# Convolution in 64x64 tiles, pair 0's centring in its weights and its y on VectorE, ssm stage by token halves, new order

## The reference

```python
y = ln_last(x) @ inproj_w                       # per position, over the 64 channels
y = depthwise_conv_3x3(y, dw2d_w) + dw2d_b      # nine taps, zero padding
s = concat([raster, reversed raster, column, reversed column] of y)
r = ln_last(s) @ ssm_in_w.T ; a, g = split(r)   # 64 -> 2 x 128
r = depthwise_conv_1x3(a * sigmoid(g), ssm_dw_w) @ ssm_out_w.T
ys = nan_clean(r) + s
m = mean of the four directions, put back in raster order
x = nan_clean(m @ outproj_w) + x
x = attention(x)     # k and v normalised per head of 4, k^T v per image, gelu of a projection
x = moe(x)           # 8 experts, hidden 256, top 2 by softmax of the gate logits
```

## Time and profile before

| | us |
|---|---|
| median of 3 runs | 89.28 (89.16 to 90.37) |
| the profiled execution, first to last instruction | 88.6 |
| PE busy | 80.8 |
| ACT busy | 58.2 |
| DVE busy | 52.4 |
| POOL busy | 23.5 |

### The profile page before, as it was taken

One profiled execution on the slowest core, in us unless ns is written; L12 is line 12 of the kernel. 1 busy time (PEld: TensorE's weight loads), 2 busy tenths in 40 slices (PEclk: granted clock), 3 DMA queues, 4 the chain that ended last, 5 costly groups with the idle time before them and its releaser, 6 DMA issues.

```text
span 88.6 us, 1470 instructions
## 1 busy us (share of the span) xinstructions
PE 80.8 (91%) x439; PEld 55.0 (62%) x439; DVE 52.4 (59%) x160; ACT 58.2 (66%) x129; POOL 23.5 (26%) x50
## 2 busy tenths in 40 slices
PE   4999998979999999799997999999999969999950
PEld 1589886548575443486783688767885638556620
DVE  3002978567996768425876768993162968036390
ACT  4547935799854766769899998954981738700910
POOL 5758000401251520600030000320004502817700
PEclk9999999999999999999999999999999999999999
DMA  0899600000000000000000000000166100355011
GB/s 19 192 391 420 281 0 0 0 0 0 0 4 4 7 0 0 0 0 0 0 7 0 0 0 0 0 0 7 40 190 189 62 0 11 115 201 162 0 59 59
DMA packets 2647, 5.36 MB, mean 60 GB/s; under 512 B 432, under 2 KB 1104, under 8 KB 2512
## 3 DMA queue, kind: packets, MB, share of 16 engines
q1 hardware_dynamic: 2496, 5.19, 17.1%
q10 hardware_dynamic: 144, 0.09, 0.4%
HBM read 4.98 MB, written 0.29 MB: 60 GB/s over the span
## 4 chain that ended last, share of the span: by engine, by line
PE 59%; DVE 11%; ACT 8%; DMA 7%; issue 5%; POOL 3%; SPq 2%; POOLq 2%; DVEq 0%
PE psM L962 7%; PE psA L773 5%; DMA wbc<-gate_mem 5%; PE psB L682 4%; PE psT L692 3%; PE psT L711 3%; DVE prod L1375 2%; PE psA L797 2%; PE psB L806 2%; PE psA L799 2%; PE psA L798 2%; PE psB L808 2%; PE psB L810 2%; PE psA L946 2%; SPq L255 2%
## 5 line engine op out<-in xcount | busy, mean ns | idle before, releaser
L558 ACT ACTIVATE hs<-psA,early 128x512 f32<-128x512 f32 x16 | 11.1, 695 | 9.0 <-PE psA L947 6.6
L962 PE MATMUL psM<-hs,w_sb 128*64 128x256 f32 x128 | 14.9, 383 | 0.1
L962 PEld LDWEIGHTS psM<-hs,w_sb 128*64 128x64 f32 x128 | 8.8, 137 | 5.8 <-issue 1.4
L558 ACT ACTIVATE hs<-psB,early 128x512 f32<-128x512 f32 x16 | 11.1, 695 | 0.0
L1375 DVE SCALAR_TENSOR_TENSOR prod<-psM,early,wbc 128x256 f32<-128x256 f32 x16 | 7.0, 475 | 6.6 <-PE psM L962 4.7
L375 POOL TENSOR_TENSOR acc<-acc,prod 128x512 f32<-128x512 f32 x5 | 6.4, 1284 | 6.2 <-DVE prod L1375 5.8
L682 PE MATMUL psB<-warm 128*128 128x512 bf16 x16 | 5.4, 489 | 1.1 <-DVE warm L1080 1.1
L946 PE MATMUL psA<-xh,w_hl 128*128 128x512 f32 x14 | 5.9, 423 | 0.0
L946 PE MATMUL psB<-xh,w_hl 128*128 128x512 f32 x14 | 5.5, 393 | 0.0
L947 PE MATMUL psA<-xl,w_hl 128*128 128x512 f32 x14 | 5.5, 392 | 0.0
L947 PE MATMUL psB<-xl,w_hl 128*128 128x512 f32 x14 | 5.5, 391 | 0.0
(11 more groups left out here) (238 smaller groups left out, 195.3 us busy)
## 6 DMA issues: line engine op xcount, KB each, us to landing
wbc<-gate_mem SPq DMA_DIRECT2D x16, 128.0 KB, 3.1
w_nat<-in_w_dram SPq DMA_DIRECT2D x1, 1024.0 KB, 7.5
late<-in_late_dram SPq DMA_DIRECT2D x1, 616.0 KB, 5.5
w_sb<-in_w_dram SPq DMA_DIRECT2D x1, 512.0 KB, 8.3
ssm_in<-in_ssm_dram SPq DMA_DIRECT2D x1, 320.0 KB, 4.2
x_sb<-in_x_chan_dram SPq DMA_DIRECT2D x2, 128.0 KB, 2.4
out_dram<-fin SPq DMA_DIRECT2D x2, 128.0 KB, 1.7
early<-in_early_dram ACTq DMA_DIRECT2D x1, 89.5 KB, 2.6
```

The costliest lines, as they stand in the source:

```text
L558: nc.scalar.activation(hs[:, n % RING, :], hidden_bank(n), ACT.Gelu, bias=cols(V_B1 + n % (E * CK))).then_inc(S["h_ok"], 1)
L962: m = nc.tensor.matmul(psM[q * C:(q + 1) * C, bank, c0:c0 + L], w2_sb[:, s % (E * CK), :], hs[:, s % RING, q * L:(q + 1) * L], start=(k == ...
```

## The change

- The convolution is done wholly in PE: nine taps for each pair, each tap as four matmuls of 64x64 with 128 columns: rows by image q, output partitions by token half t. The tap weights are no longer made on ACT as five diagonals; DVE makes `taps_c` and `taps_y`, 128x576 each, from two 64x64 unit blocks.
- Pair 0's taps have the centring in them (`taps_c`). ACT squares the convolution's result with the centred bias `conv_bc` (`conv_squares`), and `conv_normalise` on DVE writes `norm_c`. The product `centered(1, 0)` is gone. Pair 0's y, which `outproj_y(0)` still needs, is made by DVE with nine taps (`conv_tap`), spread over its list.
- Pair 1's result goes to `y_sb` by ACT (`conv_out_y`) and is centred by a product as before. Its `outproj_y(1)` becomes four tiled matmuls.
- norm_c has token half t by channel in its partitions and (image, 128 tokens) in its columns, so the ssm products, sigmoids, `gated_u` and `raster` go by token halves instead of images.
- `keep_clock(7)` moves from the first place to behind `in_product(0)`.
- The lists of all four compute engines are put in a new order, and `column` and `kv_bias_parts` are split into parts so that other work can stand between.

The core of the diff:

```diff
+            def conv_squares():
+                act.wait_ge(S["conv_ps"], 4)
+                act.wait_ge(S["bc_ok"], 1)
+                nc.scalar.activation(by_half(cen_sq[:, 0, :]), conv_banks(0), ACT.Square, bias=conv_bc[:, :])\
+                    .then_inc(Q["sq_ok"][0], 1)
+            def conv_out_y():
+                act.wait_ge(S["conv_ps"], 8)
+                act.wait_ge(S["convb_ok"], 1)
+                nc.scalar.activation(by_half(y_sb[:, 1, :]), conv_banks(1), ACT.Identity, bias=conv_b[:, :])\
+                    .then_inc(S["y_ok"], 1)
...
             in_weights()
-            conv_diagonal(0)
-            conv_diagonal(1)
+            center_squares(0, 0)
             in_bias()
-            center_squares(0, 0)
             z_weights()
             center_squares(0, 1)
             rsqrt(0, 0, LN_EPS_CONV)
-            conv_diagonal(2)
+            gate_high()
             rsqrt(0, 1, LN_EPS_CONV)
-            conv_diagonal(3)
-            conv_diagonal(4)
-            ssm_biases()
+            conv_center_bias()
+            key_norm_diagonals()
+            w1_high(0)
             ssm_weights()
-            center_squares(1, 0)
+            conv_squares()
+            conv_out_y()
             rsqrt(1, 0, LN_EPS_CONV)
             center_squares(1, 1)
-            w1_high(0)
+            ssm_biases()
+            query_weights()
             rsqrt(1, 1, LN_EPS_CONV)
...
             head_rstd(1)
             first_token_rsqrt()
+            second_half_copies()
+            query_out(1)
+            token_high(0, 0)
+            token_high(0, 1)
             nc.scalar.preload_act_table_set("gelu_and_others")
-            query_out(1)
-            second_half_copies()
-            token_high(0, 0)
             heads_with_projection(1)
-            token_high(0, 1)
-            w1_high(3)
-            proj_gelu(1)
             hidden_gelu(0)
             hidden_gelu(1)
+            proj_gelu(1)
...
+                w = (taps_c, taps_y)[h]
+                for k in range(first, last):
+                    dy, dx = divmod(k, 3)
+                    for q in range(2):
+                        rows = slice(q * C, (q + 1) * C)
+                        for t in range(T):
+                            m = nc.tensor.matmul(conv_banks(h)[t * C:(t + 1) * C, q, :].rearrange("p (y x) -> p y x", x=W),
+                                                 w[rows, k, :],
+                                                 zpad[rows, h, dy + t * H // T:dy + (t + 1) * H // T, dx:dx + W],
+                                                 start=(k == 0), stop=(k == TAPS - 1))
...
             pe.wait_ge(S["warm_ok"], 1)
-            keep_clock(7, psB[:, 0, :])
             in_bias_product()
             centered(0, 0, x_sb)
             z_weight_product()
             centered(0, 1, x_sb)
             variance(0, 0)
+            conv_bias_product()
+            variance(0, 1)
             in_product(0)
+            keep_clock(7, psB[:, 0, :])
             in_product(1)
-            variance(0, 1)
-            ssm_bias_products()
-            convolution(0, 0, 3)
-            convolution(0, 3, 5)
+            convolution(0, 0, 9)
             convolution(1, 0, 3)
-            centered(1, 0, y_sb)
-            convolution(1, 3, 5)
+            convolution(1, 3, 6)
+            convolution(1, 6, 9)
             variance(1, 0)
             centered(1, 1, y_sb)
-            outproj_y(0)
+            ssm_bias_products()
+            query_transpose()
             variance(1, 1)
             ssm_products(0)
             centered_input(0)
+            key_norm_rows()
             ssm_products(1)
             raster(0, 0)
-            query_transpose()
             raster(0, 1)
-            column(0)
+            column(0, 0, 1)
+            column(0, 1, 2)
+            column(0, 2, 3)
+            outproj_y(0)
             raster(1, 0)
             raster(1, 1)
+            column(1, 0, 1)
             outproj(0, 0)
             outproj(0, 1)
-            column(1)
-            key_norm_rows()
+            column(1, 1, 2)
+            column(1, 2, 3)
+            outproj_y(1)
             centered_with_output(0)
-            outproj_y(1)
+            outproj(1, 0)
             variance(2, 0)
-            outproj(1, 0)
             outproj(1, 1)
+            centered_input(1)
...
             output(0)
             output(1)
             output(2)
+            hidden(5)
             gate_rows(0)
             token_copies(1, 0)
             token_copies(1, 1)
-            hidden(5)
...
             output(3)
             output(4)
             output(5)
-            output(6)
-            output(7)
             gate_rows(1)
             hidden(11)
             hidden(12)
             hidden(13)
+            output(6)
+            output(7)
...
+            conv_weights(True)
+            weight_sums()
             z_out(0)
-            conv_tap(0, 0)
-            conv_tap(1, 0)
+            kv_weights()
+            conv_weights(False)
+            kv_bias_parts(0, 1)
+            conv_tap(0)
+            conv_tap(1)
             z_out(1)
...
+            conv_tap(2)
+            conv_tap(3)
+            kv_bias_parts(1, 2)
+            conv_tap(4)
+            kv_bias_parts(2, 3)
+            conv_tap(5)
+            kv_bias_parts(3, 4)
+            conv_normalise()
+            conv_tap(6)
             normalise(1, 1, norm_c)
...
             largest(1)
-            gated_pair(0)
-            gated_pair(1)
+            gated(0)
+            gated(1)
             second(1)
             gate_parts(1)
+            gated(2)
+            gated(3)
+            gated(4)
             rows_out(1)
```

More of the change, by code:

```diff
@@ L68, in conv_attention_moe @@
         psM = ps("psM", [P, PAIRS, 512])
-        psA = ps("psA", [P, PAIRS, 512])
-        psB = ps("psB", [P, PAIRS, 512])
+        psAB = ps("psAB", [P, PAIRS, 2, 512])
+        psA, psB = psAB[:, :, 0], psAB[:, :, 1]
         early = sb("early", [P, P + NVEC])
@@ L752, in in_product, with conv_bias_product @@
                              .then_inc(S["z_ps"], 1)
+            def conv_bias_product():
+                pe.wait_ge(S["convb_ok"], 1)
+                pe.wait_ge(S["center_ok"], 1)
+                nc.tensor.matmul(psB[:, 1, 4:5], center[:, :], conv_b[:, :], start=True, stop=True).then_inc(S["bc_ps"], 1)
             def ssm_bias_products():
@@ L769, in convolution @@
                     pe.wait_ge(S["border_ok"], 2)
-                for i in range(first, last):
-                    dy, dx = divmod(PE_TAPS[i], 3)
-                    pe.wait_ge(S["diag_ok"], i + 1)
-                    m = nc.tensor.matmul(psA[:, h, 0:L].rearrange("p (y x) -> p y x", x=W), conv_diag[:, i, :],
-                                         zpad[:, h, dy:dy + H, dx:dx + W], start=(i == 0), stop=(i == len(PE_TAPS) - 1))
-                if last == len(PE_TAPS):
-                    m.then_inc(S["conv_ps"], 1)
+                    pe.wait_ge(S["taps_ok"], 3 + h)
+                w = (taps_c, taps_y)[h]
[8 more added lines that the diff above has]
+                                                 start=(k == 0), stop=(k == TAPS - 1))
+                            if k == TAPS - 1:
+                                m.then_inc(S["conv_ps"], 1)
             def ssm_products(h):
@@ L783, in ssm_products @@
                 for g in (1, 0):
-                    for q, bank in enumerate((psA, psB)):
-                        rows = slice(q * C, (q + 1) * C)
-                        m = nc.tensor.matmul(bank[:, h, g * L:(g + 1) * L], ssm_w[rows, g, q, :], norm_c[rows, h, :],
+                    for t in range(T):
+                        rows = slice(t * C, (t + 1) * C)
+                        m = nc.tensor.matmul(psAB[:, h, t, g * L:(g + 1) * L], ssm_w[rows, g, t, :], norm_c[rows, h, :],
                                              start=True, stop=True)
```

293 lines of the change are left out of this document (161 added, 132 removed).

## The result

The changed kernel takes **92.81 us** (median of 4 runs, 92.13 to 93.22) against 89.66 for the kernel before (4 runs, 89.16 to 90.37): a ratio of 1.032, 95% interval 1.025 to 1.039. It is slower, and outside the range of 87.5 to 92.2. The profiled execution took 92.13, with a span of 90.4 against 88.6 before. Medians and ranges in this text are of all runs of a kernel; ratios leave out slow runs, those over 1.5% above the fastest of their kernel.

A forecast was written before the change was run, and what follows sets the result against it. A dependency chain was taken to bound the opening, PE with ScalarE and VectorE chains the middle, PE the mixture. +1.6 - 0.4 + 0.6 - 0.5 - 0.45 = +0.85 on 88.6 gives span 89.45, plus 0.68: 90.1; range 87.5 to 92.2.

The forecast's parts named there:

- The base: Whole kernel: profiled span 88.6, with the median of the runs taken as 0.68 above the span.
- the opening: Start to convolution: moving the keep-clock block starts the convolution at 10.7 instead of 9.07, +1.6, not hidden.
- the convolution to the sigmoid: Convolution's start to first sigmoid: 8.15 instead of 8.6, net -0.4.
- the middle: From the first raster on: later `outproj_y(0)`, tile changes and `w1_high` cost +0.6, bounds 0 and +0.9.
- the mixture: Mixture: pair 1's gates sooner, shorter wait at second `gate_rows`, outputs no longer stretched; together -0.45.
- the kept lag: Opening: PE's clock rises 5.8 us after its first matmul, so at 3.5 + 5.8 = 9.3.
- Four tiles at once: Convolution: all four 64x64 tiles overlap, so a tap costs 0.21 and both pairs 3.8.
- the rival of 92.1 or 93.9: Convolution: weight loads in the open, 2.0 us more (92.1), or two of four tiles at once, 3.8 more (93.9); chance 0.14.
- VectorE gives nearly the same time: Convolution to sigmoid: VectorE's list takes 16.6 before `conv_normalise`, within 0.5 of when ACT has its input.
- Into the mixture: Before `hidden(0)`: table load behind both token copies starts `hidden(0)` at 50.5, projection behind it, -0.5.
- The late clock: Opening rival: clock rises only near 10.3, convolution at 11.8, +2.7 instead of +1.6, 91.2; chance 0.13.
- The hidden opening: Opening rival: PE fast from 6.9 and middle free gives 89.0, sooner sigmoids 87.3; chance 0.23.

The follow-up runs named there:

- experiment 3: Kernel before with only the keep-clock block moved behind `in_product(0)` (and `variance(0, 1)` ahead of it in TensorE's list): 92.78 us, ratio 1.025.
- experiment 6: Changed kernel with the keep-clock block first, VectorE's `z_out` calls ahead of `weight_sums`, ssm biases early, ScalarE's list to fit: 90.34 us, ratio 1.005 to the kernel before.
- experiment 7: Changed kernel with VectorE's `z_out` calls ahead of `weight_sums` and ssm biases early, keep-clock block left behind `in_product(0)`: 92.31 us, ratio 1.028 to the kernel before.
- experiment 1: Changed kernel with its seven keep-clock products back in first place on TensorE: 92.77 us, ratio 1.028 to the kernel before.
- experiment 2: Changed kernel with the keep-clock block first and VectorE's `z_out` calls ahead of `weight_sums`, ssm biases left late: 89.67 us, ratio 0.997 to the kernel before.
- experiment 8: Block-first kernel of experiment 6 without the nine VectorE taps; `outproj_y(0)` takes pair 1's y, ahead of `variance(1, 1)`: 89.48 us, ratio 0.993 to the kernel before.
- experiment 5: Changed kernel with the mixture's old order on TensorE, VectorE and ScalarE: 92.13 us, ratio 1.017 to the kernel before.
- experiment 9: Changed kernel with `gate_rows(0)` and pair 1's token copies ahead of `hidden(5)`: 92.64 us, ratio 1.031 to the kernel before.
- experiment 10: Kernel before with the table load behind both token copies and pair 1's projection later, VectorE's list to fit: 89.39 us, ratio 0.995.
- experiment 12: Kernel before with the late table load, `gate_rows(1)` behind `output(5)`, `second(1)` ahead of `gated(2)` and `gated(3)`, `rows_out(1)` earlier: 88.73 us, ratio 0.984.

## Why the prediction was wrong, point by point

**The base, 1 us too low: the largest term that failed.** I added 0.68 to a span, the median of the runs less the profiled span of before. But a profiled execution has a time of its own. That of the changed kernel was 92.13 on a span of 90.4, 1.73 more, and the 61 executions of the kernel before beside the experiments lay 1.7 to 3.2 above their own spans (medians 2.04, 1.74 and 1.94). So the profiled 88.6 almost surely belongs to the run of 90.37 and not to the median of 89.28: the 0.68 was taken between two different executions. It was also a long span: the medians were 88.2, 88.2 and 88.3, and only 14 of the 61 were as long. With 1.73 added, my sum of 89.45 would have read 91.2.

Of the 2.7 us between 90.1 and 92.81, 1.05 is this term, 0.95 is the sum itself, and 0.68 is that the profiled execution of the changed kernel was its fastest. In the sum four terms are off: the opening by +0.3, the convolution to the sigmoid by +0.3, the middle by -0.4, the mixture by +0.85. That the middle's error takes off part of the others is luck. By the medians of the spans the change costs 90.65 less 88.3, 2.35 us or 2.7%, a little more than the 1.8 between the two profiles.

**The opening, right in place and sign, short by 0.3.** Predicted start of the convolution 10.7, measured 10.96; forecast +1.6, measured +1.89. The clock rose at about 8.5, after my 6.9 and before the 9.3 of the kept lag, and PE's first work was 2.5 later. The centring passes are still slow (the row at 4.04, 1.20 for two, and these):

```profile
L710 PE MATMUL psT<-x_sb,center x4: 634/634/774, 4.0 to 5.9; 128*128 128x256 f32 x4
```

Experiments 3, 6 and 7 confirm the price: 1.6 in the opening of the kernel before, 2.0 in time with the rest equal. What I did not see is that in the changed kernel VectorE's list would cost as much if the block were gone (experiment 1).

**Four tiles at once, right.** I took 0.21 a tap. 72 passes took 2.20, or 0.24 a tap with entering and leaving. The rows of single instructions:

```profile
L802 PEld LDWEIGHTS psAB<-zpad,taps_c x72: 129/133/133, 11.0 to 12.8; 64*64 64x64 f32 x72
L802 PE MATMUL psAB<-zpad,taps_c x72: 267/268/320, 11.0 to 12.9; 64*64 64x128 f32 x72
```

A load record of 133 ns with each pass, and a pass every 31 ns: nothing is paid in the open, and the rival of 92.1 or 93.9 is out. In the Trainium skill, "TensorE: Matmul & The Clock Gate", the section on packing small matmuls lets a load overlap running matmuls only where the row group differs. Here every second matmul has the rows of the one before it, and with loads of 133 ns and a pass every 31 ns the trace does not agree.

**From the convolution to the sigmoid, -0.4 predicted, -0.11 measured.** I counted ScalarE's way at 8.15 and let pair 1's taps follow pair 0's at once; it took 8.50. The step that failed is "VectorE gives nearly the same time": VectorE's list came in ahead of ScalarE's way and not beside it. Pair 1's taps had to wait for `z_out(1)`, which ended at 13.10, and the 1/sqrt of pair 0 came 5.89 after the convolution's start, where it is 5.66 in experiments 2 and 6. The list held `conv_normalise` back too: it began at 17.58, right behind a bias part, though its 1/sqrt was done at 16.85. That delay was covered, since it ended at 18.06 and the late biases released the ssm products 0.12 later (L481, to 18.18). With VectorE's list mended and the biases late the stretch is 8.27, near my 8.15; with the biases early as well it is 7.86 (experiments 2 and 6).

**The middle, +0.6 predicted, +0.17 measured.** The sign is right and the size too large. Which of the terms I counted (tile changes, `outproj_y(0)`, `w1_high`) cost nothing I did not separate. Up to pair 0's gelu the changed kernel is 0.17 behind (24.76 against 24.59), and pair 0's late y can make that much: it costs 0.4 there in the mended kernel (experiment 8).

**Into the mixture, -0.5 predicted, -0.55 measured.** Right. The load at 52.32 hides behind `hidden(0)`.

**The mixture, -0.45 predicted, +0.4 measured.** This is the step with the wrong sign. The two parts that I counted came true, in part: the second `gate_rows` waits 0.51 (before 0.74), and the outputs behind it go at full rate, 64 passes in 7.13, 0.11 each, where 48 took 5.70. What I counted at nothing was `gate_rows(0)`, one expert later. I compared its 8.6 us to the product at 68.73, but the first pair of products needs the transfer too, and in the kernel before they already waited for it, 0.29 us at 66.16:

```profile
66.16 0.88 DVE L1375 SCALAR_TENSOR_TENSOR prod<-psM,early,wbc 128x256 f32<-128x256 f32 x2 [0.29 <-DMA wbc<-gate_mem]
```

There the cover was 6.0 us and used up. In the changed kernel these two products wait 2.16, until 69.53, and `output(4)` with them. It starts at 70.46, 1.62 behind `output(3)` at 68.84, whose eight passes take 0.91: 0.71 late. Not all of it is the later call. Counted from the raster product, the first `gate_rows` is 0.65 later than before, its products 1.60. The other 0.95 is the transfer: the second of the eight reads of `wbc` took 3.98 us to land in the changed kernel and 3.03 before, and about 4.0 in each of experiments 1, 2 and 6, which also have `gate_rows(0)` late, against 3.0 to 3.2 in experiments 5, 9, 10 and 12, which have it early. What delays it stays open. Experiment 9 gives 0.3 back, since other waits come up. In the old order TensorE waits as long at the second gates and for a late output (experiment 5). The only kernel that gained behind the raster product, 1.2, has early first gates, early second gates and the late table load together (experiment 12).

**The rivals.** The late clock (91.2) was the nearest in time, but not by its mechanism: the convolution started at 10.96 and not at 11.8. The hidden opening and the tiles are out. What happened was the forecast's own mechanism in the opening, on a base one microsecond too low, with VectorE's list underrated and a wrong sign in the mixture.

**Still open.** Three kernels with one and the same opening list (before, experiments 10 and 12) started their convolution at 9.07, 8.01 and 8.71, and in the record of the granted clock it rose at 6.9, 4.5 and 6.2. What decides this in one execution I did not find. It hides differences of 0.5% here (experiments 5, 9, 10). And the block-first kernel of experiment 6 should lie 0.35 below the kernel before, by 0.75 saved and 0.4 paid; its median span is 88.4 against 88.2. What its start costs, for instance by the 0.81 us of tap weights now ahead of `z_out(0)` on VectorE, wasn't tried.

## What to carry to other kernels

Make the sum on the profiled execution's own time, and ask whether that execution was typical: a profiled span less the median of other runs is not an offset. When work is moved later in a list, look up the first instruction that uses its result and whether it waits already; the cover is what that row leaves, not what a later one does. And where two causes stand in one queue's shadow (here the filler in TensorE's list and work that is not due in VectorE's), undoing one can show nothing: undo both, and each in the kernel before as well. When a profile shows something striking, as the slow clock of experiment 1, ask whether it lies on the chain and whether the other executions had it.

## What the runs showed of the hardware

- TensorE fell from 2.4 to 1.2 GHz in the middle of the opening, behind a stretch in which it had mostly stood still (busy 1.04 of 3.30 us), and 72 passes then cost 3.35 us, not 2.20. This was in one of four executions of experiment 1; the others show a mean granted clock of 0.996 or more.
- fp32 passes in four 64x64 tiles of 128 columns ran every 31 ns (72 in 2.20 us), with a weight load each.
- 130 more matmuls did not lengthen the time outside the span (1.83 against 2.04 us in the medians).
- One small VectorE step on 128x4 values (L1343, L1413) took 1.08 us in the kernel before and 0.47 and 0.48 in the changed kernel and in experiment 12; its neighbours take 0.19. In all three it began while a GpSimd addition ran and ended 0.02 to 0.03 us after it (71.04 behind 71.02, 71.23 behind 71.21, 67.14 behind 67.11). I did not test the cause.
